# Scatter phase: the two buffers around the block transposes laid out with pairs of experts and pairs of indices innermost

## The reference, cut to what matters

```python
# groups of g = 32 tokens; 32 experts x 4 sets = 128 slots (e, s)
perm = (logits == max(logits, axis=tokens))          # [n, t, e, s]
permuted = einsum('bntd,bntes->bnesd', grouped, perm)  # each slot picks a token of the group
inner = relu(einsum('bnesd,esdf->bnesf', permuted, W1) + b1)   # f = 32
result_permuted = einsum('bnesf,esdf->bnesd', inner, W2) + b2  # d = 512
result = einsum('bnesd,bntes->bntd', result_permuted, perm)    # back to the tokens
```

## Time and profile before

| | |
|---|---|
| median of three runs | 3041.65 us (3038.51 to 3043.23) |
| the profiled execution | 3036.95 us |
| its span, first to last instruction | 3035.2 us |
| busy over the span | TensorE matmul 92%, weight load 74%, VectorE 73%, ScalarE 58%, GpSimd 54% |
| granted TensorE clock, mean | 0.973 of full speed |
| scatter phase | from about 2480 us to the end |
| block transposes, line 1700 | 128, busy for 539.0 us |

### The profile page before, as it was taken

One profiled execution on the slowest core, in us unless ns is written; L12 is line 12 of the kernel. 1 busy time (PEld: TensorE's weight loads), 2 busy tenths in 40 slices (PEclk: granted clock), 3 DMA queues, 4 the chain that ended last, 5 costly groups with the idle time before them and its releaser, 6 DMA issues.

```text
span 3035.2 us, 135365 instructions
## 1 busy us (share of the span) xinstructions
PE 2799.8 (92%) x59836; PEld 2250.2 (74%) x59836; DVE 2220.8 (73%) x2743; ACT 1749.4 (58%) x3552; POOL 1628.4 (54%) x2447
## 2 busy tenths in 40 slices
PE   8999999999999999999999999996878868887877
PEld 6888888888888888888888888875667754444443
DVE  6777777777777777777777777774444449999998
ACT  5665666666666566665666656653333335565654
POOL 4666766766667676666666766761101104344434
PEclk9999999999999999999999999998999979998988
DMA  4222222222222222222222222226544435566554
GB/s 152 74 75 74 76 74 77 77 79 70 71 78 74 78 76 73 76 74 77 77 73 76 74 73 78 72 59 211 142 130 124 114 127 172 176 201 202 175 173 137
DMA packets 262713, 316.38 MB, mean 104 GB/s; under 512 B 28000, under 2 KB 184032, under 8 KB 260464
## 3 DMA queue, kind: packets, MB, share of 16 engines
q1 hardware_dynamic: 252176, 297.55, 32.2%
q10 hardware_dynamic: 9952, 10.17, 1.0%
HBM read 194.31 MB, written 113.31 MB: 101 GB/s over the span
## 4 chain that ended last, share of the span: by engine, by line
PE 87%; issue 6%; DVE 4%; DMA 1%; SPq 1%; POOL 1%; ACT 0%; POOLq 0%; ACTq 0%; DVEq 0%
PE a_proj L991 39%; PE a_mix L991 11%; PE s_ps L1719 6%; PE g_pick_ps L1465 5%; PE a_scan L1105 5%; PE s_ps L1740 5%; PE s_ps L1735 3%; DVE g_picked L1394 3%; PE a_scan L1082 3%; PE a_scan L1069 2%; PE g_acc_ps L1489 2%; PE a_mix L1057 2%; PE a_misc L1049 1%; PE a_misc L1123 1%; DMA part_dram<-res 1%
## 5 line engine op out<-in xcount | busy, mean ns | idle before, releaser
L1700 DVE STREAM_TRANSPOSE s_turned<-s_stage 128x2048 f32<-128x2048 f32 x128 | 539.0, 5225 | 2.0 <-ACT s_stage L1678 2.0
L991 PE MATMUL a_proj<-wdh,xTh 128*128 128x512 f32 x1024 | 421.6, 412 | 6.0 <-issue 4.2
L991 PE MATMUL a_proj<-wdh,xTl 128*128 128x512 f32 x1024 | 402.5, 393 | 0.0
L991 PE MATMUL a_proj<-wdl,xTh 128*128 128x512 f32 x1024 | 401.3, 392 | 1.2 <-issue 1.2
L823 DVE COPY_PREDICATED scan_in<-mask,a_scan 64x512 f32<-64x512 uint32 x512 | 382.3, 747 | 16.1
L1678 ACT COPY s_stage<-s_ps 128x1024 f32<-128x1024 f32 x256 | 247.1, 1018 | 210.5 <-DVE s_turned L1700 107.6
L472 POOL TENSOR_TENSOR yv<-yt,dx 128x512 f32<-128x512 f32 x128 | 189.2, 1478 | 292.2 <-DVE yt L863 292.2
L464 POOL TENSOR_TENSOR dx<-xs,d_row 64x512 f32<-64x512 f32 x256 | 331.5, 1295 | 15.1
L1657 POOL TENSOR_TENSOR s_out<-s_out,s_part 128x512 f32<-128x512 f32 x128 | 164.8, 1288 | 325.6 <-ACT s_out L1684 324.5
L639 ACT ACTIVATE scan_in<-CT,hsel 64x128 f32<-64x128 f32 x1024 | 326.1, 388 | 4.8
L603 ACT ACTIVATE raw<-a_proj,rs 128x272 f32<-128x272 f32 x128 | 62.5, 489 | 427.8 <-PE a_proj L991 427.8
(11 more groups left out here) (153 smaller groups left out, 7362.7 us busy)
## 6 DMA issues: line engine op xcount, KB each, us to landing
x<-in_x_dram SPq DMA_DIRECT2D x128, 256.0 KB, 2.6
xn_dram<-xn SPq DMA_DIRECT2D x128, 256.0 KB, 2.4
part_dram<-res SPq DMA_DIRECT2D x128, 256.0 KB, 2.5
g_xn<-xn_dram SPq DMA_DIRECT2D x512, 64.0 KB, 2.2
s_part<-part_dram SPq DMA_DIRECT2D x128, 256.0 KB, 3.6
out_dram<-s_out SPq DMA_DIRECT2D x128, 256.0 KB, 2.9
xr<-in_xT_dram SPq DMA_DIRECT2D x126, 256.0 KB, 2.9
s_inner<-inner_dram SPq DMA_DIRECT2D x32, 512.0 KB, 5.3
```

The lines of the kernel that those rows point to most:

```text
L991: last = nc.tensor.matmul(out, lhs[a], rhs[c], start=(k == 0 and n == 0), stop=(k == nk - 1 and n == 2))
L1700: nc.vector.transpose(turned[m % 2][:, :, cols].rearrange("p n d -> p d n"), stage[m % 2][:, :, cols].rearrange("p e d -> p d e")).then_in ...
```

## The change

The last axis of both buffers becomes a pair. `stage` is now [partition, pair of experts 0..15, feature, expert of the pair], and `turned` is [partition, pair of groups 0..15, feature, group of the pair]; their sizes and places stay. Expert 8i + 4j + 2h + r is in pair 4i + 2j + h at place r. ScalarE writes the same values in the same order into these places; a run of features, 256 adjacent words before, is now 256 words with a step of two. The transpose reads and writes pairs of adjacent words, and then hops by 512 words (2 KB); before, it hopped by 256 words (1 KB) at each word. The matmul on `turned` reads its 256 features with a step of two words. No instruction, wait or DMA is added, taken away or moved.

```diff
-    stage = [sb(f"stage{i}", [P, EX // 4, DH], at=a) for i, a in enumerate((AT_XNT, AT_W1 + 32768))]
-    turned = [sb(f"turned{i}", [P, SG, DH], at=AT_PICKED + 32768 * i) for i in range(2)]
+    stage = [sb(f"stage{i}", [P, EX // 8, DH, 2], at=a) for i, a in enumerate((AT_XNT, AT_W1 + 32768))]
+    turned = [sb(f"turned{i}", [P, SG // 2, DH, 2], at=AT_PICKED + 32768 * i) for i in range(2)]
...
-        places = stage[m % 2][:, 8 * i:8 * i + 8, :].rearrange("p (j r) d -> p r j d", r=4)
+        places = stage[m % 2][:, 4 * i:4 * i + 4, :, :].rearrange("p (j h) d r -> p h r j d", h=2)
         for h in range(2):
-            nc.scalar.copy(places[:, 2 * h:2 * h + 2, :, :], bank[:, pair(u, h), :, :]).then_inc(w2_cp, 1)
+            nc.scalar.copy(places[:, h, :, :, :], bank[:, pair(u, h), :, :]).then_inc(w2_cp, 1)
...
-                nc.vector.transpose(turned[m % 2][:, :, cols].rearrange("p n d -> p d n"),
-                                    stage[m % 2][:, :, cols].rearrange("p e d -> p d e")).then_inc(turn_cp, 1)
+                nc.vector.transpose(turned[m % 2][:, :, cols, :].rearrange("p n d i -> p d n i"),
+                                    stage[m % 2][:, :, cols, :].rearrange("p e d i -> p d e i")).then_inc(turn_cp, 1)
...
-                                            turned[m % 2][:, g * (SG // GPT) + 2 * x + t, :], start=False, stop=True,
+                                            turned[m % 2][:, g * (SG // GPT // 2) + x, :, t], start=False, stop=True,
```

## The result

| | before | after |
|---|---|---|
| median | 3040.08 us (4 runs, 3037.68 to 3043.23) | 2931.22 us (4 runs, 2929.93 to 2932.16) |
| ratio | | 0.9641, 95% interval 0.9624 to 0.9658 |
| profiled execution | 3036.95, span 3035.2 | 2931.32, span 2929.5 |
| granted TensorE clock, mean | 0.973 | 0.989 |

The change made the kernel 3.6% faster, 109 us. The forecast was 2902 us; the measured time is inside the range (2887 to 2962) and 29 us above the forecast.

A forecast was written before the change was run, and what follows sets the result against it. VectorE's transposes bound the scatter phase; with them faster, 116 units at TensorE's 3.095 us, the tail and 2 us of DMA gain 136.8 us, giving 2900 to 2905, forecast 2902 us, range 2887 to 2962.

The forecast's parts named there:

- What bounds the kernel: Scatter phase: VectorE, busy 100.00 us of 100, is the bound; its four transposes set the step of 16.9 us.
- Item 1, the transposes: VectorE's transposes in the scatter phase fall from 4.23 to 2.30 us each; anything up to 3.09 us gives the same time.
- The rival that a four-byte transpose costs double whatever the layout: VectorE's transposes don't get faster, since four-byte words and not hops set their price; time as before, 3041 us; chance 0.07.
- Item 2, the evictions: ScalarE's copies from PSUM, now writing every second word, stay at 1018 ns; upper bound 2.04 us.
- The cover of about a quarter: ScalarE's first eviction ends some 0.5 us before TensorE's next apply_w2 needs it, so it may grow by a quarter free.
- Item 3, the matmuls on `turned`: TensorE's 16 matmuls per unit, reading every second word, stay at 1.07 us; no cover, each 10% costs 12 us.
- Item 4, what is late next: Scatter phase after the change: gather, GpSimd and DMA keep up; only the w2 reload is crowded, charged 2 us once.
- The pace of 3.095 us: TensorE's time per unit in the scatter phase without stalls, 12.38 us a step, taken for 116 units: 359.0 us.
- The start: The sum begins after apply_w2 of unit 12 at 2513.21 us in the profiled execution, where the first stall goes.
- the partly paid cases: Matmuls on `turned` cost 30% more, 2939 us, or transposes take 3.6 us, 2961 us; chance 0.13.
- the case on the other side: ScalarE's evictions double to 2.04 us through their stepped writes, a step takes 18.3 us, time 3084 us; chance 0.09.
- The formula: ScalarE's time per unit: two evictions less 0.1 us plus a copy out of 0.60; 4.58 us with evictions of 2.04.

The follow-up runs named there:

- two single-sided runs: Pairs in `stage` only, then pairs in `turned` only, the other buffer as in the kernel before: 2980.4 and 2994.3 us, beside 3043.6 for the kernel before.

## Why the prediction was right, point by point

- *What bounds the kernel*: right. The two single-sided runs bear it out: their times follow the transposes. VectorE's transposes set the step, and with them faster the step went to TensorE's pace; the clock followed, 0.91 to 1.00.
- *Item 1, the transposes*: forecast 2.30 us, measured 2.22. The rival that a four-byte transpose costs double whatever the layout is refuted by the same number, 1.08 ns an element. The small transpose's 1.5 ns an element was not its rate in long streams: at 1.08 ns its 28 further elements take 30 of the 42 ns (199 - 157), and the rest must be a fixed part. What the prediction did not know, and the two single-sided runs show, is that one hopping side alone keeps it at 3.7 us, above the 3.09 us that decide.
- *Item 2, the evictions*: "no change" was wrong in size (1127 to 1151 ns for 1018) and right in effect. The cover of about a quarter held it: the run with contiguous writes, at 1017 ns, is not clearly faster.
- *Item 3, the matmuls on `turned`*: 1.07 us was forecast, 1.11 measured. With the linear price given there (12 us for each 10%) 3.7% are 4 us, and 4.0 were found.
- *Item 4, what is late next*: this is the term that was mis-sized. The crowded reload of w2 was seen and charged at 2 us; it cost 6.0 to 7.3. The prediction charged it once, as data that come late, and charged nothing for the DMA share of 0.78 that it worked out for the other steps. The data did come in time: from 2500 to 2900 us of the profiled execution the only wait for a DMA is one of 0.2 us. What came late, by the reading above, were instructions. In all 19.5 to 26.0 us were lost in place of 2, the larger part of the 33 us, and up to 1.7 us of it for each fall of the clock (an estimate: 3.4 us at half speed), one or two in each of the three executions.
- *The pace of 3.095 us*, taken from three units in a row of a step in which TensorE then rested, was a pace without such stalls; the sum multiplied it by 116 as if none would fall among them.
- *The start*: the sum took the gather phase of one execution, which was the earliest of twelve. Those 8 us lie within what chance gives.
- *The range*: it held because it reached to 2962 us for the partly paid cases, not because the stalls were in it. The forecast's own spread, 2888 to about 2915 us, misses the 2931; that part of the hit is luck.
- *The rivals*: the case on the other side has the mechanism that was given, but it needs a step of four words. The predicted threshold was an eviction of 1.86 us, and at 2.16 us the kernel was only level with the one before. The formula was wrong by its overlap: it gives 2 x 2.16 - 0.1 + 0.60 = 4.82 us for a unit of ScalarE, and the unit was 4.19, since two evictions took 3.91 to 4.02 us together and the copy out overlaps them in the records.

## What to carry to other kernels

A buffer that one engine must cross against the grain can give the crossing engine runs of two words at a small price for those who go along the grain (here 11 to 16% of a write that had cover, 4% of a read that had none); runs of four bought nothing more here and cost them double. Both sides of the crossing need it. When an engine's rest is removed, ask what its rests were covering: here, with a DMA share of 0.73, a TensorE with 168 short instructions in 3.1 us lost 5 to 7% to stalls that no semaphore explains, and a pace read from a burst of three or four units does not contain them.

## What the runs showed of the hardware that was not expected

- A write by ScalarE with a step of two words costs 11 to 16% (1127 median, 1151 to 1179 ns mean, against 1017), a read by TensorE 4% (1.11 us for 1.07). With a step of four words the write takes 2157 ns, 2.1 times, and the read 2.00 us, 1.9 times.
- Reading PSUM with a hop to another bank at each element shows no price on ScalarE (1017 ns for 1024 elements, 1018 without the hop).
- The stalls without a releaser mostly end 1.4 us after a packet of the instruction queue, and what is lost between units 12 and 127 falls from 22.8 to 6.6 us as the DMA share of that stretch falls from 0.73 to 0.49.
- A stall of 2.29 us inside one group of matmuls was followed by 3.4 us at a granted clock of 0.50, during which 16 matmuls took 1.94 us in place of 1.11.
